# The histogram of the clipped edges, moved from the head of the fourth layer to its closing

## The chip, the cores and the metric

The kernel runs on one core of a Trainium2 chip. The metric is the device time of one execution in microseconds (us); the number compared is the median of several runs. PE is TensorE, DVE is VectorE, ACT is ScalarE, POOL is GpSimd, SP is the engine that issues most transfers.

## The reference, cut to what matters

The network takes four images of 128 channels and 1024 tokens through four layers and a graph step with experts. The fourth layer (`_L3_attn_ref`) is a global attention with 8 heads of 16, a local attention over a window of 5, and two small networks:

```python
x_global = global_mha(x, g_in_w, g_in_b, g_out_w, g_out_b, H_GLOBAL)
x_local = local_mha(x, t_in_w, t_in_b, t_out_w, t_out_b, H_LOCAL)
x_comb = jnp.concatenate([x_global, x_local], axis=-1)
x_fused = jax.nn.silu(x_comb @ fus_w1.T + fus_b1) @ fus_w2.T + fus_b2
x = layer_norm(x + x_fused, gn_g, gn_b)
x_ffn = jax.nn.silu(x @ ffn_w1.T + ffn_b1) @ ffn_w2.T + ffn_b2
x = layer_norm(x + x_ffn, fn_g, fn_b)
```

The graph step behind it softmaxes over the edges that arrive at each of M = 4096 nodes:

```python
e = jax.nn.leaky_relu(a_src[src] + a_dst[dst], negative_slope=0.2)
denom = jax.ops.segment_sum(jnp.exp(e - e_max[dst]), dst, num_segments=M)
```

Edge indices can lie beyond M. A source beyond M is clipped to the last node, so all such edges carry the same message, and the kernel needs of them only how many arrive at each node: a histogram over 4096 nodes, `k.count`.

## The kernel before

**The histogram.** An earlier stage leaves in DRAM (`last_digits`) the target of each clipped edge as two base-64 digits, 1024 slots in each of 128 partitions. For a stretch of slots DVE writes one-hot rows: one `is_equal` for each of the 64 digit values, over both digits at once (`one_hots`, L2510, into `f_hot` or `f_hot_late`). PE multiplies low by high one-hots, two 64x64 products a slot pair, accumulated in PSUM (`multiply`, L2060). A stretch is called a tally. There are nine: five of 128 slots (`EARLY`) ahead of the layer's first image, and four of 96 slots (`LATE`) beside that image. In all 1024 such matmuls and 576 `is_equal`s. A sum over the two halves and a small transposition give `k.count` (L2525, L2086, L2528). It is read only in the graph step.

**The layer** is one stage, `fourth_layer_stream`. Every engine runs its own list in order, and semaphores tie them. The main line is 256 steps, 64 an image. A step makes two score tiles (L2156, PE) into the ring of two PSUM banks, whose row maxima DVE takes (L2492); two transposed score tiles (L2183), of which ACT makes exponentials (L2375); and half a visit of products with the values (L2202, "mix"). The operands of the scores are the stacks, `f_stacks`, loaded by SP from DRAM (L2698, 12 transfers a group of two heads, 48 in the first load).

**Beside it** run smaller programs that yield turn numbers, two turns a step: `pre(b)` (norm, projections and bf16 parts of image b), `local(b)`, and `tail(b)` (output projection, the two networks and three norms of image b). `Beside.turn` lets every program with a due turn issue; programs in the order of their list on ties. `tail(b)` starts at turn 128(b+1), stretched by `TAIL_PACE` 1.1, so `tail(3)` lies behind the last step: the closing. Nothing else but the end of `local(3)` was due there. `tail` uses one PSUM bank, `x0`: PE fills it, ACT or DVE empties it, and only then PE fills it again. The late tallies accumulated in `x0`'s bank, so `tail(0)` waited for `tallied`.

**Ahead of the steps** each engine ends `pre(0)`. Then PE ran the five early tallies into `f_O` (L2071), with one small matmul for `f_o_bias`, and DVE the 320 `is_equal`s for them; then came 32 score tiles with their maxima, then step 0. POOL waited for the early tallies (L2651) before it cleared `f_pads`, which shares their memory. SP loaded the digits (L2717, L2718), then parts and stacks.

## Time and profile before

| | us |
|---|---|
| median of 3 runs | 2576.82 (2575.90 to 2578.19) |
| profiled execution, its own time | 2575.91 |
| its span | 2574.1 |
| PE, DVE, ACT, POOL busy | 1915.4, 1592.9, 1024.6, 723.4 |
| last part of `pre(0)` on PE to first score tile | 1320.8 to 1377.0 |
| first score tile to step 0 | 1377.0 to 1404.4 |
| images 0, 1, 2, 3 (ends of their last group) | 1623.0, 1816.0, 2012.3, 2186.4 |
| the closing (`tail(3)`) | 2186.4 to 2298.4 |
| graph step and experts | to 2574.1 |

The places are in us from the span's start. The own time is 1.8 above the span: what lies around it. Busy shares over the whole span say little here, since each stretch has its own limit; the stretches are read one by one.

### The profile page before, as it was taken

Reading aid. Unit: us, or ns where it says so; the run is one execution under the profiler, and the core shown is the slowest. Engines: PE = TensorE matmul, PEld = TensorE weight load, DVE = VectorE, ACT = ScalarE, POOL = GpSimd, SP = SyncE. Lnnn points to the kernel's source line nnn. Section 1 sums busy time; section 2 is a strip of 40 time slices with the busy share of each in tenths; the row PEclk is TensorE's granted clock in tenths of the full one; section 3 lists DMA queues with packets and bytes.
Section 4 is the critical chain, followed back from the end, with each engine's and each line's share of the span. In section 5 each row is a group of like instructions: output and inputs, shape, how many; then the busy total and the mean of one; then the engine's idle time right before and its main releaser. Section 6 shows DMA issues by size and latency. Waiting matters only on the chain. (4 is left out here: it accounts for less than half of the span.)

```text
span 2574.1 us, 26674 instructions
## 1 busy us (share of the span) xinstructions
PE 1915.4 (74%) x8906; PEld 866.5 (34%) x8906; DVE 1592.9 (62%) x3660; ACT 1024.6 (40%) x1662; POOL 723.4 (28%) x693
## 2 busy tenths in 40 slices
PE   1594786787589566599978889887887887338595
PEld 1121321322233134456654333222322222124355
DVE  3477768768677775547667666566566563115567
ACT  0242142224304116445511544765765665224251
POOL 2300620440171041034450211233233123127730
PEclk7696887789689777789955998998998997659797
DMA  3300300300030000021020010110110100014100
GB/s 97 90 3 25 90 0 19 80 17 19 10 87 1 23 3 0 1 97 20 16 68 15 27 28 15 38 41 15 39 41 15 28 3 4 12 59 52 10 5 34
DMA packets 55807, 80.26 MB, mean 31 GB/s; under 512 B 17217, under 2 KB 28983, under 8 KB 55424
## 3 DMA queue, kind: packets, MB, share of 16 engines
q1 hardware_dynamic: 45158, 69.14, 9.0%
q10 hardware_dynamic: 6426, 7.99, 1.4%
q0 software_dynamic: 4096, 1.58, 1.3%
q8 instruction: 62, 1.02, 0.2%
q14 instruction: 65, 0.53, 0.1%
HBM read 50.13 MB, written 24.68 MB: 29 GB/s over the span
## 5 line engine op out<-in xcount | busy, mean ns | idle before, releaser
L2492 DVE TENSOR_REDUCE f_half_max<-f_ring 128x1 f32<-128x512 f32 x512 | 339.1, 686 | 286.7 <-PE f_ring L2156 284.3
L2375 ACT ACTIVATE f_probs<-f_ST 128x512 f32<-128x512 f32 x512 | 294.6, 597 | 262.6 <-PE f_ST L2183 259.0
L2156 PE MATMUL f_ring<-f_stacks 96*128 96x512 bf16 x512 | 215.3, 422 | 46.1 <-DVE f_half_max L2492 39.9
L772 DVE TENSOR_REDUCE att_half_max<-att_ring 128x1 f32<-128x512 f32 x256 | 161.2, 684 | 101.1 <-PE att_ring L659 92.2
L2183 PE MATMUL f_ST<-f_stacks 99*128 99x512 bf16 x512 | 207.1, 410 | 11.8 <-ACT f_probs L2375 11.8
L755 ACT ACTIVATE att_probs<-att_ST 128x1024 f32<-128x1024 f32 x128 | 129.3, 1023 | 155.9 <-PE att_ST L684 155.7
L2202 PE MATMUL f_O<-f_probs,f_v_ext 128*32 128x512 f32 x1024 | 157.5, 691 | 0.1
L3208 POOL DMA_INDIRECT ti_row<-features,slot_from x128 | 127.0, 992 | 56.4 <-issue 56.4
L659 PE MATMUL att_ring<-stacks 96*128 96x512 bf16 x256 | 104.5, 473 | 47.3 <-DMA stacks<-parts_dram 25.6
L684 PE MATMUL att_ST<-stacks 96*128 96x512 bf16 (+1 forms) x512 | 137.7, 398 | 0.0
L1242 DVE TENSOR_TENSOR loc_weighed<-loc_wide,l_pad 128x512 f32<-128x512 f32 x200 | 124.8, 684 | 19.9 <-PE loc_wide L1196 15.3
L702 PE MATMUL att_O<-att_probs,v_ext 128*64 128x512 f32 x512 | 130.5, 635 | 6.7 <-DVE att_den L791 6.7
L2156 PEld LDWEIGHTS f_ring<-f_stacks 96*128 96x128 bf16 x512 | 50.8, 99 | 249.5 <-DVE f_half_max L2492 168.3
L1739 ACT ACTIVATE bm_h<-bm_ps,bn 128x512 f32<-128x512 f32 x128 | 99.5, 777 | 78.2 <-PE bm_ps L1706 72.9
L1762 POOL TENSOR_TENSOR bm_h<-bm_h,bm_mix 128x512 f32<-128x512 f32 x64 | 82.0, 1303 | 159.6 <-ACT bm_h L1739 88.5
L1224 POOL TENSOR_TENSOR loc_partial<-loc_partial,loc_weighed 128x512 f32<-128x512 f32 x88 | 110.0, 1271 | 15.3 <-DVE loc_weighed L1242 11.8
L1053 POOL MEMSET loc_padded<- 104x1296 f32 x4 | 4.7, 1177 | 387.3 <-POOLq L43 387.3
L1202 PE MATMUL loc_acc<-loc_weighed,turned 128*128 128x512 f32 x208 | 111.2, 619 | 0.0
L2763 PE MATMUL gm_ps<-xn_cm,x 128*128 128x512 f32 x128 | 65.9, 643 | 44.8 <-ACT turned L2811 35.0
L1019 PE MATMUL loc_ps<-loc_prod,place 128*32 128x512 f32 (+1 forms) x208 | 56.8, 713 | 31.2 <-DVE loc_prod L1081 31.2
L2352 ACT CAST f_stacks<-f_ring 3x512 bf16<-3x512 f32 x64 | 36.9, 577 | 97.7 <-PE f_ring L2168 97.2
L684 PEld LDWEIGHTS att_ST<-stacks 96*128 96x128 bf16 (+1 forms) x512 | 49.4, 102 | 75.5 <-issue 17.5
(589 smaller groups left out, 3698.1 us busy)
## 6 DMA issues: line engine op xcount, KB each, us to landing
f_stacks<-f_parts SPq DMA_DIRECT2D x192, 64.0 KB, 2.2
parts_dram<-l_parts SPq DMA_DIRECT2D x8, 768.0 KB, 3.6
stacks<-parts_dram SPq DMA_DIRECT2D x24, 256.0 KB, 9.4
stacks<-parts_dram ACTq DMA_DIRECT2D x24, 256.0 KB, 10.5
f_parts<-f_parts SPq DMA_DIRECT2D x8, 768.0 KB, 3.4
es_raw<-L_ffn_edge_index SPq DMA_DIRECT2D x8, 512.0 KB, 4.1
bm_mix<-mix SPq DMA_DIRECT2D x8, 512.0 KB, 8.7
xn_cm<-x SPq DMA_DIRECT2D x1, 2048.0 KB
```

Of the source, the lines that this page charges most:

```text
L684: last = nc.tensor.matmul(ST[:, s % 2, n * BANK:(n + 1) * BANK], k.stacks[0:rows, 1, per * h + j, m * P:(m + 1) * P], k.stacks[0:rows, 0, ...
L702: last = nc.tensor.matmul(O[at:at + width, :], k.v_ext[:, m, h, :], probs[:, s % probs_ring, n * BANK:(n + 1) * BANK], start=(m == 0), sto ...
L755: nc.scalar.activation(probs[:, s % probs_ring, :], ST[:, s % 2, :], ACT.Exp).then_inc(probs_ready, 1)
L772: nc.vector.tensor_reduce(half_max[:, h % 2, t, n:n + 1], ring[:, i % RING], AX.X, ALU.max, negate=True).then_inc(reduced, 1)
L1202: nc.tensor.matmul(acc[:, n], w_out, weighed[:, (i - LAG) % RING], start=(j == 0), stop=False).then_inc(summed, 1)
L1242: nc.vector.tensor_tensor(o_, a, v, ALU.mult).then_inc(weighed_ready, 1)
L2156: nc.tensor.matmul(ring[:, i % RING], f.stacks[0:STACK, 0, at, t * P:(t + 1) * P], f.stacks[0:STACK, 1, at, n * BANK:(n + 1) * BANK], star ...
L2183: nc.tensor.matmul(ST[:, i % HALVES], f.stacks[0:STACK + 3, 1, h % HEADS, m * P:(m + 1) * P], f.stacks[0:STACK + 3, 0, h % HEADS, n * BANK ...
L2202: last = nc.tensor.matmul(O[at:at + 32, :], f.v_ext[:, h // HEADS % 2, m, h % HEADS, :], f.probs[:, s % PROBS, n * BANK:(n + 1) * BANK], s ...
L2375: nc.scalar.activation(f.probs[:, s % PROBS, n * BANK:(n + 1) * BANK], ST[:, i % HALVES], ACT.Exp).then_inc(probs_ready, 1)
L2492: nc.vector.tensor_reduce(f.half_max[:, h % 2, t, n:n + 1], ring[:, i % RING], AX.X, ALU.max, negate=True).then_inc(reduced, 1)
L3208: self.nc.gpsimd.indirect_dma_start(self.row[:, j, :], None, self.k.features, bass.IndirectOffsetOnAxis(ap=self.k.slot_from[:, j:j + 1], a ...
```

## The change

All nine tallies leave the head of the layer. In their place stand eight tallies of 128 slots in the closing, beside `tail(3)`: 1024 matmuls as before, 512 `is_equal`s. One-hots stand in `f_hot`, two buffers, now laid over `f_stacks` (first buffer) and over `f_v_ext` and `f_probs` (second buffer). So tally 0 waits for the last transposed scores, tally 1 for the last mix, and from tally 2 on DVE waits until PE is done with the buffer. The product stands in the ring's banks, the digits in the second third of `f_xn`, `total` and `place` in `f_qk`. The turns come from a table, `TALLY_TURNS`: DVE makes tally s between entries s and s+1, in pieces of 4 values; PE multiplies it between entries s+1 and s+2, in pieces of 8 matmuls; both are stretched by 1.1 as the tail is. SP's digits transfer is one, at turn 384. `tail(0)`, the first mix, and POOL's clearing of `f_pads` lose their waits.

```diff
-    EARLY, EARLY_TALLIES, LATE, LATE_TALLIES, LATE_TURNS = 128, 5, 96, 4, 28
+    TALLY, TALLIES = 128, 8
+    TALLY_TURNS = (0, 13, 25, 35, 48, 56, 72, 83, 93, 104)
...
+        with ExitStack() as last:
+            self.hot = last.enter_context(sbuf(nc, "f_hot", [P, 2, 2, 2, 64, self.TALLY // 2], BF16))
         self.stacks = sb("f_stacks", [P, 2, self.HEADS, N], BF16)
         self.v_ext = sb("f_v_ext", [P, 2, NT, self.HEADS, 32])
+        self.probs = sb("f_probs", [P, self.PROBS, N])
...
+    def tally_turn(s, share):
+        lo, hi = (f.TALLY_TURNS[min(i, f.TALLIES + 1)] for i in (s, s + 1))
+        return lo + (hi - lo) * share
...
-        if tally is not None:
-            programs.append((0, tally()))
...
+        if tally is not None:
+            programs.append((B * TURNS, paced(tally(), f.TAIL_PACE)))
...
         def first():
-            for s in range(f.EARLY_TALLIES):
-                yield 22 + 2 * s
-                if s == 0:
-                    nc.tensor.matmul(ST[:, 0, 0:1], k.turned[:, k.t_g_out, :], k.cols[:, C_G_IN + 2:C_G_IN + 3],
-                                     start=True, stop=True).then_inc(carried, 1)
-                pe.wait_ge(hot_ready, 64 * (s + 1))
-                multiply(O, f.hot[:, s % 2], range(f.EARLY // 2), s == 0, s == f.EARLY_TALLIES - 1).then_inc(multiplied, 1)
+            yield 22
+            nc.tensor.matmul(ST[:, 0, 0:1], k.turned[:, k.t_g_out, :], k.cols[:, C_G_IN + 2:C_G_IN + 3],
+                             start=True, stop=True).then_inc(carried, 1)
 
         def tally():
-            half, per = f.LATE // 2, 4
-            for s in range(f.LATE_TALLIES):
+            half, per = f.TALLY // 2, 4
+            for s in range(f.TALLIES):
                 for g in range(half // per):
-                    yield f.LATE_TURNS * s + 15 + g
+                    yield tally_turn(s + 1, g * per / half)
                     if g == 0:
-                        pe.wait_ge(hot_ready, 64 * (f.EARLY_TALLIES + s + 1))
+                        pe.wait_ge(hot_ready, 64 * (s + 1))
+                        pe.wait_ge(reduced, count["s"])
+                        pe.wait_ge(rows_off, count["r"])
...
             for n in range(NC2):
                 yield 24 + 2 * n
-                if b == 0 and n == 0:
-                    pe.wait_ge(tallied, 1)
...
-            if v == 0:
-                pe.wait_ge(counted, 2)
...
         before.finish()
-        dve.wait_ge(digits_in, 32)
-        for s in range(f.EARLY_TALLIES):
-            if s >= 2:
-                dve.wait_ge(multiplied, s - 1)
-            one_hots(f.hot[:, s % 2], f.digits[:, :, s * f.EARLY:(s + 1) * f.EARLY], range(64))
-            if s == 2:
-                dve.wait_ge(carried, 1)
...
+        dve.wait_ge(carried, 1)
...
-        pool.wait_ge(multiplied, f.EARLY_TALLIES)
         nc.gpsimd.memset(f.pads[:], 0.0).then_inc(cleared, 1)
...
+        def digits():
+            yield 0
+            normed.wait(sp, 1, 2 * NT)
+            sp.dma_start(f.digits, k.digits_dram).then_inc(digits_in, 16)
```

PE at the head of the layer. Before, with the last matmul of `pre(0)` first (L2005), the early tallies (L2060) and the first score tiles (L2156):

```order
L2005 MATMUL f_side<-turned,xn_cm 128x128 x8
L2068 MATMUL f_ST<-cols,turned 128x1
L2060 MATMUL f_O<-f_hot 64x64 x640
L2156 MATMUL f_ring<-f_stacks 128x512 x32
L2168 MATMUL f_ring<-ident_b,f_shift_parts 3x128 x16
```

Now (the change moves line numbers by a few; L2152 is the score tile):

```order
L2005 MATMUL f_side<-turned,xn_cm 128x128 x8
L2066 MATMUL f_ST<-cols,turned 128x1
L2152 MATMUL f_ring<-f_stacks 128x512 x32
L2164 MATMUL f_ring<-ident_b,f_shift_parts 3x128 x16
```

The 640 matmuls between the two are gone.

PE in the closing, before: output projection (L2117), first network (L2096, L2105), turned tokens (L1985), second network, turned tokens, features (L2142):

```order
L2202 MATMUL f_O<-f_probs,f_v_ext 32x512 x8
L2117 MATMUL f_side<-f_o,turned 128x512 x2
L2096 MATMUL f_side<-f_both,turned 128x512 x8
L2105 MATMUL f_side<-turned,f_hid 128x128 x16
L1985 MATMUL f_side<-ident,f_x_415 128x128 x8
L2096 MATMUL f_side<-xn_cm,turned 128x512 x4
L2105 MATMUL f_side<-turned,f_hid 128x128 x16
L1985 MATMUL f_side<-ident,f_x_415 128x128 x8
L2142 MATMUL f_side<-w_gat,xn_cm 128x24 x8
```

Now the tallies' matmuls (L2060) stand between them. The first part, up to the first turned tokens:

```order
L2060 MATMUL f_ring<-f_hot 64x64 x112
L2113 MATMUL f_side<-f_o,turned 128x512
L2060 MATMUL f_ring<-f_hot 64x64 x32
L2113 MATMUL f_side<-f_o,turned 128x512
L2060 MATMUL f_ring<-f_hot 64x64 x32
L2094 MATMUL f_side<-f_both,turned 128x512 x2
L2060 MATMUL f_ring<-f_hot 64x64 x48
L2094 MATMUL f_side<-f_both,turned 128x512 x2
L2060 MATMUL f_ring<-f_hot 64x64 x56
...
L2103 MATMUL f_side<-turned,f_hid 128x128 x8
L2060 MATMUL f_ring<-f_hot 64x64 x128
```

In the lines left out, the pieces are 32, 56 and 16. The second part, from the second network to the end:

```order
L2060 MATMUL f_ring<-f_hot 64x64 x32
L2094 MATMUL f_side<-xn_cm,turned 128x512
L2060 MATMUL f_ring<-f_hot 64x64 x64
L2103 MATMUL f_side<-turned,f_hid 128x128 x8
L2060 MATMUL f_ring<-f_hot 64x64 x24
L2103 MATMUL f_side<-turned,f_hid 128x128 x8
L2060 MATMUL f_ring<-f_hot 64x64 x280
L1985 MATMUL f_side<-ident,f_x_413 128x128 x8
L2084 MATMUL f_ring<-f_qk 128x32 x2
```

Pieces of 16 and 32 stand ahead of these. No piece stands behind the last 280.

DVE in the closing. Before, from the reciprocal of the softmax sums (L2478) through the first norm:

```order
L2478 RECIPROCAL f_inverse<-f_den 128x64
L2462 SCALAR_TENSOR_TENSOR f_hid<-f_bent,f_straight 128x512 x4
L2472 TENSOR_TENSOR f_xn<-f_side,f_xn 128x512 x2
L2395 BN_STATS f_moments_tail<-f_xn 128x6 x8
L2399 BN_AGGR f_norm_tail<-f_moments_tail 128x2 x8
```

Now, with the one-hots (L2504) between, here from the second residual (L2466) on:

```order
L2466 TENSOR_TENSOR f_xn<-f_side,f_xn 128x512
L2389 BN_STATS f_moments_tail<-f_xn 128x6 x4
L2504 TENSOR_SCALAR f_hot<-f_xn 128x4x64 x8
L2389 BN_STATS f_moments_tail<-f_xn 128x6 x4
L2504 TENSOR_SCALAR f_hot<-f_xn 128x4x64 x4
L2393 BN_AGGR f_norm_tail<-f_moments_tail 128x2 x8
L2504 TENSOR_SCALAR f_hot<-f_xn 128x4x64 x8
```

Twenty one-hots have come between the residual and the end of the first norm's moments; ahead of them, 68 stand before the reciprocal and 104 between it and the first `f_hid`.

## Rows read from the trace of the kernel before

**Rows 1.** Busy time by engine in four stretches, with the granted clock (PEclk).

```profile
core 0: us, PE busy (x) PEld busy (x) DVE busy (x) ACT busy (x) POOL busy (x), PEclk, DMA share, GB/s
1320.00:1377.00 57.00, 54.83 (x646) 54.45 (x646) 30.32 (x193) 2.74 (x3) 23.46 (x5) 0.50 0.27 83
1404.00:1623.00 219.00, 189.50 (x1070) 66.78 (x1069) 147.76 (x492) 106.12 (x186) 35.46 (x31) 0.88 0.07 21
1623.00:1816.00 193.00, 157.40 (x795) 53.69 (x794) 117.42 (x281) 121.97 (x230) 57.15 (x76) 0.96 0.11 32
2186.00:2298.00 112.00, 41.55 (x128) 23.25 (x124) 17.52 (x73) 24.12 (x47) 19.89 (x44) 0.60 0.03 7
```

**Rows 2.** Timeline of PE at the head: start, duration, work, [idle before <- releaser].

```profile
1320.77 21.66 PE L2060 MATMUL f_O<-f_hot 128*64 128x64 bf16 x256
1344.60 32.42 PE L2060 MATMUL f_O<-f_hot 128*64 128x64 bf16 x384 [2.17 <-DVE f_hot L2510]
1376.96 1.03 PE L2156 MATMUL f_ring<-f_stacks 96*128 96x512 bf16 x2
```

**Rows 3.** Timeline of DVE at the head of the layer.

```profile
1295.39 17.62 DVE L2510 TENSOR_SCALAR f_hot<-f_digits 128x256 bf16<-128x256 bf16 x128
1331.81 12.73 DVE L2510 TENSOR_SCALAR f_hot<-f_digits 128x256 bf16<-128x256 bf16 x64 [18.80 <-PE f_O L2060]
1355.67 8.80 DVE L2510 TENSOR_SCALAR f_hot<-f_digits 128x256 bf16<-128x256 bf16 x64 [2.34 <-PE f_O L2060]
1377.60 11.05 DVE L2492 TENSOR_REDUCE f_half_max<-f_ring 128x1 f32<-128x512 f32 x16 [13.13 <-PE f_ring L2156]
```

**Rows 4.** Timeline of SP's queue: the load of the stacks.

```profile
1332.45 24.45 SPq L2698 DMA_DIRECT2D f_stacks<-f_parts  x48
```

**Rows 5.** DMA issues by line at the head: KB each, median us to landing.

```profile
f_stacks<-f_parts SPq DMA_DIRECT2D x48, 64.0 KB, 2.2
```

**Rows 6.** Groups by line and form in image 0: busy, mean ns.

```profile
L2510 DVE TENSOR_SCALAR f_hot_late<-f_xn 128x192 bf16<-128x192 bf16 x256 | 44.1, 239 | 0.0
L2060 PE MATMUL f_side<-f_hot_late 128*64 128x64 bf16 x384 | 42.6, 367 | 0.0
```

**Rows 7.** Timeline of PE in image 0: one piece and what follows it.

```profile
1433.35 0.88 PE L2060 MATMUL f_side<-f_hot_late 128*64 128x64 bf16 x8
1434.16 1.12 PE L1999 MATMUL f_side<-xn_cm,turned 128*128 128x512 f32 x2
```

**Rows 8.** Timeline of ACT: the copies that end image 0 and image 1.

```profile
1623.00 0.58 ACT L2360 COPY f_raw<-f_O 128x512 f32<-128x512 f32 x1 [0.43 <-PE f_O L2202]
1816.00 0.58 ACT L2360 COPY f_raw<-f_O 128x512 f32<-128x512 f32 x1 [0.43 <-PE f_O L2202]
```

**Rows 9.** Timeline of PE in the closing.

```profile
2184.09 2.21 PE L2202 MATMUL f_O<-f_probs,f_v_ext 128*32 128x512 f32 x16
2203.79 2.08 PE L2117 MATMUL f_side<-f_o,turned 128*128 128x512 f32 x2 [17.48 <-POOL f_o L2619]
2209.65 3.54 PE L2096 MATMUL f_side<-f_both,turned 128*128 128x512 f32 x4 [0.87 <-ACT f_both L163]
2214.70 1.96 PE L2096 MATMUL f_side<-f_both,turned 128*128 128x512 f32 x4 [1.51 <-ACT f_straight L163]
2227.98 2.02 PE L2105 MATMUL f_side<-turned,f_hid 128*128 128x128 f32 x16 [0.88 <-DVE f_xn L2472]
2262.48 3.75 PE L2105 MATMUL f_side<-turned,f_hid 128*128 128x128 f32 x16 [0.88 <-DVE f_xn L2472]
2290.42 1.12 PE L1985 MATMUL f_side<-ident,f_x 128*128 128x128 f32 x4 [24.19 <-ACT f_x L2237]
```

**Rows 10.** Timeline of POOL: one subtraction at the head, the softmax scaling in the closing.

```profile
1310.99 4.00 POOL L2587 TENSOR_TENSOR f_qk<-f_qk,f_parts 128x1024 f32<-128x1024 f32 x1 [12.54 <-ACT f_parts L2256]
2201.39 2.34 POOL L2619 TENSOR_TENSOR f_o<-f_o,f_x 128x1024 f32<-128x1024 f32 x1 [27.00 <-DMA f_x<-f_inverses]
```

**Rows 11.** What line L2587 took in all: minimum, median, maximum in ns.

```profile
L2587 POOL TENSOR_TENSOR f_qk<-f_qk,f_parts x8: 2121/2128/4004, 1311.0 to 1860.0; 128x1024 f32<-128x1024 f32 x8
```

More of the change, by code:

```diff
@@ L1829, in __init__ @@
         self.features = sb("f_features", [P, NT, FEAT])
[L1830 to L1838 removed]
+        self.digits = self.xn[:, 1].rearrange("p t n -> p (t n)").bitcast(BF16).rearrange("p (d n) -> p d n", d=2)
+        self.total = self.qk[:, 0, 0:256].rearrange("p (o n q) -> p o n q", o=2, q=2)
+        self.place = self.qk[:, 0, 256:320]
         self.raw = sb("f_raw", [P, 2, BANK])
@@ L1847, in __init__ @@
         self.att_t = sb("f_att_t", [3 * self.ROWS, N], BF16)
-        with ExitStack() as late:
-            self.hot_late = late.enter_context(sbuf(nc, "f_hot_late", [P, 2, 2, 64, self.LATE // 2], BF16))
         self.both = sb("f_both", [P, 2, N])
@@ L2512, in tally @@
         def tally():
-            per = 5
-            for s in range(f.LATE_TALLIES):
+            yield tally_turn(0, 0)
+            split.wait(dve, B - 1)
+            for half in range(2):
+                r = slice(64 * half, 64 * half + 64)
+                nc.vector.tensor_copy(f.place[r, :], k.ident[r, r]).then_inc(tally_made, 1)
+            nc.vector.memset(f.total, 0.0).then_inc(tally_made, 1)
+            dve.wait_ge(digits_in, 16)
+            per = 4
+            for s in range(f.TALLIES):
                 for g in range(0, 64, per):
-                    yield f.LATE_TURNS * s + 1 + g // per
+                    yield tally_turn(s, g / 64)
                     if g == 0:
-                        dve.wait_ge(multiplied, f.EARLY_TALLIES + s)
-                    one_hots(f.hot_late, f.digits_late[:, :, s * f.LATE:(s + 1) * f.LATE], range(g, min(g + per, 64)))
-            yield f.LATE_TURNS * f.LATE_TALLIES + 2
-            dve.wait_ge(multiplied, f.EARLY_TALLIES + f.LATE_TALLIES)
-            dve.wait_ge(counted, 2)
+                        if s == 0:
+                            dve.wait_ge(st_ready, NC2 * len(steps))
+                            dve.wait_ge(reduced, count["s"])
+                        elif s == 1:
+                            dve.wait_ge(mixed_ready, len(steps) // VISIT)
+                        else:
+                            dve.wait_ge(multiplied, s - 1)
+                    one_hots(f.hot[:, s % 2], f.digits[:, :, s * f.TALLY:(s + 1) * f.TALLY], range(g, g + per))
+            yield tally_turn(f.TALLIES + 1, 0) + 2
+            dve.wait_ge(multiplied, f.TALLIES)
+            dve.wait_ge(tally_made, 3)
             for odd in range(2):
-                x = f.total[:, odd, :, odd]
-                nc.vector.tensor_tensor(x, x0.psum[:, 0:64], x, ALU.add).then_inc(counted, 1)
-            yield f.LATE_TURNS * f.LATE_TALLIES + 6
+                nc.vector.tensor_copy(f.total[:, odd, :, odd], ring[:, 0, 0:64]).then_inc(counted, 1)
+            yield tally_turn(f.TALLIES + 1, 0) + 6
             dve.wait_ge(spread_out, 1)
-            nc.vector.tensor_copy(k.count[:], x0.psum[:, 64:64 + MT]).then_inc(tallied, 1)
+            nc.vector.tensor_copy(k.count[:], ring[:, 1, 0:MT]).then_inc(tallied, 1)
         def laps():
```

32 lines of the change are left out of this document (7 added, 25 removed).

## Prediction, made before the changed kernel was run

> **What bounds the kernel now.** No engine is busy over the whole span, so the reader goes stage by stage: busy times by stretch, then the timelines of the engines that wait there. Three stretches carry the histogram or will.
>
> At the head of the layer PE and DVE hand tallies to each other, and PE is the slower. It runs 256 matmuls in 21.66 us and 384 in 32.42 [rows 2]: 0.0845 us each, 10.8 for a tally of 128. DVE makes 64 one-hots in 8.8 us, 0.1375 each, and otherwise waits for PE, 18.80 us once [rows 3]. The first score tile starts at 1376.96, on the heels of the last tally matmul [rows 2]. The stacks that it reads were loaded long before: SP issued 48 transfers in 24.45 us from 1332.45 [rows 4], each landing 2.2 us after its issue [rows 5]. So this stretch is paced by the histogram alone.
>
> In image 0 both PE (189.5 of 219 us) and DVE (147.8) are fuller than in image 1 (157.4 and 117.4 of 193), though image 1 has a tail beside it and image 0 has none [rows 1]. The surplus is the late tallies.
>
> In the closing all engines are nearly empty: PE 41.6 of 112 us, DVE 17.5 [rows 1]. It is one chain, PE, ACT, DVE, POOL in turn, with gaps on PE from 0.88 us inside the networks to 17.48 and 24.19 ahead of the output projection and the last turned tokens [rows 9].
>
> **Part 1, the head: -36.3 us.** Gone from PE are 640 matmuls, from DVE 320 one-hots. What is late next is the load of the first group's 12 transfers. SP issues one each 24.45/48 = 0.51 us, the twelfth at 1332.45 + 11 x 0.51 = 1338.1; issued by 1338.5 and landed 2.2 later, at 1340.7 [rows 4, 5]. The first score tile starts there and not at 1376.96 [rows 2]: 36.3 saved. The 32 tiles and their maxima keep their pace, 11.05 us for 16 on DVE [rows 3]. The remaining 36 transfers end near 1359, and step 0, at 1404.4 - 36.3 = 1368, is the first to want the second group. SP's own queue loses two digit transfers ahead of `pre(0)`; the parts' transfers wait for POOL, so nothing moves. POOL clears `f_pads` earlier, and nobody waits for it. Bounds: 34 if the transfers land as late as 1343; 37 if the load is a little faster.
>
> **Part 2, image 0: -44 us.** Gone are 48 pieces of 8 matmuls. A piece takes 0.81 us to the next start [rows 7]: 48 x 0.81 = 38.9 on PE. DVE loses 256 one-hots, 44.1 us busy [rows 6]. They lie side by side, so at most the larger counts in full. Image 0's steps take 1623.0 - 1404.4 = 218.6 us [rows 8]. From PE's side: 218.6 - 38.9 = 180 if its 30 us of waiting stay, and some of that waiting is for maxima that stood behind one-hots. From DVE's side 218.6 - 44.1 = 174.5. From a like image: image 1 took 193.0 [rows 8] with `pre`, `local` and a tail; the tail's PE work in the closing is 41.6 us, mostly at half clock [rows 1], so 20 to 25 at full clock; that leaves 168 to 173. I take 174.5: 44 saved. Bounds: 26, if image 0 only falls to image 1's 193, and 52, if it reaches 167.
>
> **Part 3, the closing: +41 us.** This is the sum with the most in it, and I walk through PE's list as it is built. PE has 1024 x 0.0845 = 86.5 us of tallies to place beside 41.6 of tail [rows 1, 2]. Idle there are 70 us, but they must be idle at the right places, since PE runs in order: a projection whose input is ready waits for the piece in front of it.
> - Tally 0: DVE may start at the last transposed scores, 2184.2 [rows 9], and needs 8.8; PE starts it at 2193.0 and has run 112 matmuls (9.5 us) by 2202.5, ahead of the projection at 2203.79 [rows 9]. It costs nothing: it fills the 17.48.
> - POOL's scaling at 2201.39 [rows 10] now meets DVE's one-hots of tally 1, which run to 2202.6. In the head the same meeting cost POOL: 4.00 us for an instruction with a median of 2.13 [rows 10, 11], ending 2 us after DVE's burst of 17.62 us from 1295.39 [rows 3]. So it starts at 2202.6: +1.2.
> - Output projection and first network: between these eight operations stand 32, 32, 48, 56, 32, 56 and 16 tally matmuls, 272 x 0.0845 = 23.0 us. The operations are two projections of 2.08, four of 3.54 and two of 3.75 at half clock [rows 9]: 25.8. PE never waits in here, so the stretch lasts 48.8. Before it lasted 2230.00 - 2203.79 = 26.2 [rows 9]: +22.6.
> - First norm on DVE: 8, 4 and 8 one-hots between its instructions, 20 x 0.1375: +2.8. Beside the norm PE runs tally 3 (10.8) in a gap of at least 12: nothing.
> - Second network: here gaps of 1.51 (0.88 ahead of the last) face pieces of 16 and 32 at the turned tokens (+1.7), three of 32, each 2.7 against 1.51 plus 0.35 of overlap with the end of the operation before (+0.9 each, +2.7), 64 (+4) and 24 (+1.3): +9.7.
> - Second norm: 28 one-hots (3.9) and a wait until PE is done with tally 5 (1.3): +5.1.
> - Tallies 6 and 7, 256 matmuls or 21.6 us on PE, fall into the 24.19 ahead of the last turned tokens [rows 9]: nothing. They end some 5 us before the tokens are there. If that cover were gone, each us over it would count in full.
>
> 1.2 + 22.6 + 2.8 + 9.7 + 5.1 = 41.4. Bounds: 23, with the clock as in the first rival, and 50, if each of some 17 re-entries costs the 0.81 - 8 x 0.0845 = 0.13 us that a piece in image 0 costs over the steady rate [rows 2, 7] and POOL loses a burst of 0.1375 x 36 = 5 to DVE once more.
>
> The new digits transfer on SP at turn 384 lands during image 3, 100 us and more before it is read; queued behind it are the moves of one group, which wait for PE anyway. Nothing.
>
> **Sum.** Own time 2575.9 - 36.3 - 44 + 41.4 = 2537.0; the median of the runs is 0.9 above that execution. **Forecast 2538 us.**
>
> **The clock, and a page that speaks for more.** The tally matmuls did not raise PE's clock: from 1320 to 1377 it was busy for 54.8 of 57 us with them and the granted clock was 0.50 throughout, the level of 1.2 GHz [rows 1]. In the closing it rose once, after the four-matmul projection at 2209.65: 3.54 us before it and 1.96 after for the same form [rows 9]. I therefore price the tail's operations at half clock throughout. The Trainium skill, "TensorE: Matmul & The Clock Gate", section "Why this matters for your kernels", says that an engine kept continuously busy gets and keeps the full clock. By it the closing, where PE now hardly idles, would run at 2.4 GHz. The trace does not agree for these narrow matmuls; whether mixed with wide ones they let it rise, no row of the closing shows.
>
> **The port, and a page.** In the head, a POOL instruction was held until DVE's one-hots ended (above), which is where my 1.2 us come from. The Trainium skill, "SBUF — State Buffer", section "Who interferes with whom", says that the second to issue is blocked until the first instruction finishes, a single instruction. By it POOL would wait for one one-hot, 0.1 us, and the sum would be 1.1 lower. The row has 1.9 us, and I follow it.
>
> **Rivals.**
> - *The clock comes back in the closing.* Mixed with wide projections the pieces may let it rise; in image 0 pieces ran at full clock, 1.12 us for a projection right behind one [rows 7]. Then the first stretch loses four times 3.54 - 1.96 and twice 3.75 - 2.02 and half of the two projections, 11.6 us, and the second network about 7: closing +23. 2519 us. Against it stands the head's 0.50. 17%.
> - *Image 0 is held by its other chain.* `pre(1)` and `local(0)` pass one bank between PE, ACT, DVE and POOL, at a speed that tallies do not set. Then it falls only to image 1's 193.0: 26 instead of 44. 2556 us. Against it: image 1 has a tail as well. 13%.
> - *The load is late.* If the first tiles in fact waited for all 48 transfers, to 1359, the head gives 18: 2556 us. The change would not do what it says there. PE's wait names 12 only. 5%.
> - *Slower: nothing hides.* PE runs strictly in order. If each tally delays the chain by its full length, because one-hots and matmuls are each ready only when the next operation of the tail is too, then the closing costs 86.5 + 8.8 = 95, 15 more than the 80 that parts 1 and 2 give: 2592 us. It decides from the point where less than 15 us of tally work fall into idle time. The 17.48 and 24.19 [rows 9] alone hold 31. 4%.
>
> **How the numbers follow.** Forecast 61%, its own range 2524 to 2550 (image 0 by 8 either way, the closing by 9). The range that should hold 8 in 10 reaches to the clock's 2519 and to the 2556 of the two middle rivals, with a little for the tails: 2514 to 2558. A measurement of this kernel can tell about 0.2%, 5 us. All cases but the last and a small middle lie far below: faster 0.95, same 0.01, slower 0.04.
>
> **What would show it.** First score tile near 1341; step 0 near 1368; image 0 ending near 1543, the closing starting near 2106 and lasting 153 instead of 112; PE without idle time between the output projection and the second projection of the network, at a granted clock near 0.50; tally 7 over some 5 us before the last turned tokens. I am wrong if image 0 lasts 190 or more, if PE waits for one-hots inside the networks, if the last tally runs into the last turned tokens, or if the clock is at 1.00 in there.

## Result and the profile after

The changed kernel takes 2506.8 us (median of 4 runs, 2505.3 to 2514.1) against 2577.5 (median of 4, 2575.9 to 2581.1): a ratio of 0.9729, interval 0.9707 to 0.9751, or 70.7 us less. The forecast was 2538, its range 2514 to 2558. The sign was right, and the gain was 31 us larger than foretold.

The profiled execution takes 2505.7 us, its span is 2503.9. The two spans, cut at the same events (first norm of the layer on DVE, first ACT exponential of the attention, the last copy of O of each image, the last copy of features):

| stretch | before, us | after, us | difference | forecast |
|---|---|---|---|---|
| ahead of the layer | 1290.4 | 1285.1 | -5.3 | 0 |
| head | 114.7 | 77.3 | -37.4 | -36.3 |
| image 0 | 217.9 | 159.5 | -58.4 | -44 |
| image 1 | 193.0 | 193.1 | +0.1 | 0 |
| image 2 | 196.3 | 196.2 | -0.1 | 0 |
| image 3 | 174.0 | 167.7 | -6.3 | 0 |
| closing | 111.7 | 148.1 | +36.4 | +41.4 |
| behind the layer | 276.1 | 276.8 | +0.7 | 0 |
| span | 2574.1 | 2503.9 | -70.2 | -38.9 |

Busy time by engine in the head up to the first score tile, in image 0, image 1, image 3 and the closing of the changed kernel (compare [rows 1]):

```profile
core 0: us, PE busy (x) PEld busy (x) DVE busy (x) ACT busy (x) POOL busy (x), PEclk, DMA share, GB/s
1285.10:1334.20 49.10, 14.75 (x34) 7.42 (x34) 4.22 (x21) 12.24 (x20) 21.64 (x19) 0.54 0.15 50
1361.70:1521.90 160.20, 136.76 (x681) 36.87 (x680) 105.93 (x232) 103.11 (x186) 34.62 (x31) 0.95 0.09 28
1521.90:1715.10 193.20, 158.36 (x795) 53.99 (x795) 117.45 (x282) 122.01 (x231) 57.16 (x76) 0.95 0.11 32
1911.30:2078.90 167.60, 142.87 (x702) 45.96 (x700) 89.68 (x228) 106.24 (x202) 46.02 (x59) 0.92 0.05 13
2078.90:2227.40 148.50, 131.54 (x1152) 111.64 (x1152) 86.00 (x574) 24.70 (x48) 24.25 (x44) 0.65 0.02 6
```

The timeline of PE at the head, after (compare [rows 2]): the wait is now for the stacks' load, as foretold.

```profile
1315.06 0.43 PE L2066 MATMUL f_ST<-cols,turned 128*128 128x1 f32 x2
1334.24 1.03 PE L2152 MATMUL f_ring<-f_stacks 96*128 96x512 bf16 x2 [18.76 <-DMA f_stacks<-f_parts]
```

The timeline of SP's queue there, after, up to 1337 us (compare [rows 4]):

```profile
1326.89 10.43 SPq L2689 DMA_DIRECT2D f_stacks<-f_parts  x22
```

The timeline of POOL there, after: the subtraction that took 4.00 us [rows 10] is back at the line's median [rows 11], since no one-hots run beside it.

```profile
1305.64 2.12 POOL L2579 TENSOR_TENSOR f_qk<-f_qk,f_parts 128x1024 f32<-128x1024 f32 x1 [12.52 <-ACT f_parts L2250]
```

The timeline of PE in the closing, after (compare [rows 9]):

```profile
2085.64 9.64 PE L2060 MATMUL f_ring<-f_hot 128*64 128x64 bf16 x112 [6.76 <-DVE f_hot L2504]
2097.28 2.08 PE L2113 MATMUL f_side<-f_o,turned 128*128 128x512 f32 x2 [2.00 <-POOL f_o L2611]
...
2107.05 3.78 PE L2094 MATMUL f_side<-f_both,turned 128*128 128x512 f32 x4
2110.76 4.29 PE L2060 MATMUL f_ring<-f_hot 128*64 128x64 bf16 x48
2114.98 3.44 PE L2094 MATMUL f_side<-f_both,turned 128*128 128x512 f32 x4
2118.35 4.94 PE L2060 MATMUL f_ring<-f_hot 128*64 128x64 bf16 x56
2123.22 3.15 PE L2094 MATMUL f_side<-f_both,turned 128*128 128x512 f32 x4
2126.30 2.89 PE L2060 MATMUL f_ring<-f_hot 128*64 128x64 bf16 x32
2129.12 1.98 PE L2094 MATMUL f_side<-f_both,turned 128*128 128x512 f32 x4
...
2143.00 10.92 PE L2060 MATMUL f_ring<-f_hot 128*64 128x64 bf16 x128
2154.97 1.12 PE L1985 MATMUL f_side<-ident,f_x 128*128 128x128 f32 x4 [1.05 <-ACT f_x L2231]
...
2203.89 10.97 PE L2060 MATMUL f_ring<-f_hot 128*64 128x64 bf16 x128 [1.10 <-DVE f_hot L2504]
2219.44 1.11 PE L1985 MATMUL f_side<-ident,f_x 128*128 128x128 f32 x4 [4.59 <-ACT f_x L2231]
```

From the output projection at 2097.28 no row carries a wait until 2154.97: every operation of the network now stands behind a piece of tallies, and the last tally ends 4.6 us ahead of the last turned tokens. Both were foretold. What was not is the same form, four wide matmuls, in 3.78, 3.44, 3.15 and 1.98 us. The granted clock says why: it changes between its two levels, 0.50 (1.2 GHz) and 1.00 (2.4 GHz), while PE never pauses; a figure between them is the mean of both. Over the first and second of the four, and over a piece and the fourth:

```profile
2107.05:2110.83 3.78, 3.78 (x8) 1.24 (x6) 0.00 (x0) 0.00 (x0) 0.00 (x0) 0.50 0.00 0
2114.98:2118.35 3.37, 3.37 (x7) 0.96 (x5) 0.66 (x5) 0.00 (x0) 0.00 (x0) 0.56 0.03 5
2126.30:2129.12 2.82, 2.82 (x34) 2.72 (x33) 1.33 (x7) 1.29 (x2) 0.00 (x0) 1.00 0.01 3
2129.12:2131.03 1.91, 1.91 (x6) 0.67 (x5) 1.91 (x16) 0.00 (x0) 0.00 (x0) 1.00 0.00 0
```

Over the third it was 0.61, over the pieces between the first three 0.86 and 0.85.

Three entries of the table were to be explained: image 0 (14 us more than forecast), the closing (5 us less added than forecast) and two stretches that the change does not touch, ahead of the layer and image 3, 11.6 us together.

### The profile page after: what moved, and what is told of

The parts are those of the page before. It is cut to its first block and busy times, and to the rows that moved or that the text cites. A ratio compares the mean times of both kernels' runs of the same rounds, so it can differ in the third digit from the quotient of the medians.

```text
span 2503.9 us, 26613 instructions
## 1 busy us (share of the span) xinstructions
PE 1892.9 (76%) x8906; PEld 869.7 (35%) x8906; DVE 1573.4 (63%) x3594; ACT 1021.7 (41%) x1662; POOL 714.1 (29%) x693
## 5 line engine op out<-in xcount | busy, mean ns | idle before, releaser
L2152 PE MATMUL f_ring<-f_stacks 96*128 96x512 bf16 x512 | 212.1, 415 | 54.5 <-DVE f_half_max L2486 28.1
L2152 PEld LDWEIGHTS f_ring<-f_stacks 96*128 96x128 bf16 x512 | 50.4, 99 | 258.8 <-DVE f_half_max L2486 162.6
L659 PE MATMUL att_ring<-stacks 96*128 96x512 bf16 x256 | 103.7, 471 | 46.5 <-DMA stacks<-parts_dram 25.9
L2060 PE MATMUL f_ring<-f_hot 128*64 128x64 bf16 x1024 | 90.5, 366 | 7.9 <-DVE f_hot L2504 7.9
L2060 PEld LDWEIGHTS f_ring<-f_hot 128*64 128x64 bf16 x1024 | 87.1, 272 | 22.4 <-issue 12.7
L2504 DVE TENSOR_SCALAR f_hot<-f_xn 128x256 bf16<-128x256 bf16 x512 | 72.3, 220 | 28.7 <-issue 14.7
```

The lines of the kernel that those rows point to most:

```text
L2060: last = nc.tensor.matmul(bank[64 * a:64 * a + 64, 0:64], low, high, start=(start and m == ms[0]), stop=(stop and m == ms[-1]), tile_posit ...
L2152: nc.tensor.matmul(ring[:, i % RING], f.stacks[0:STACK, 0, at, t * P:(t + 1) * P], f.stacks[0:STACK, 1, at, n * BANK:(n + 1) * BANK], star ...
```

## Experiments on image 0: do the two engines' tallies lie side by side, or add?

The forecast rested on the sentence that PE's matmuls and DVE's one-hots lie side by side, "so at most the larger counts in full". Three kernels made from the one before take the late tallies apart. In `late_none` both edits are made, in each of the others one. PE's edit leaves one pair of matmuls of each tally, on the identity:

```diff
                 for g in range(half // per):
                     yield f.LATE_TURNS * s + 15 + g
...
-                    last = multiply(x0.psum, f.hot_late, range(per * g, per * (g + 1)), s == 0 and g == 0,
-                                    s == f.LATE_TALLIES - 1 and g == half // per - 1)
+                    if g < half // per - 1:
+                        continue
+                    for a in range(2):
+                        last = nc.tensor.matmul(x0.psum[64 * a:64 * a + 64, 0:64], k.ident_b[:, 0:64], k.ident_b[:, 0:64],
+                                                start=(s == 0), stop=(s == f.LATE_TALLIES - 1), tile_position=(0, 64 * a))
```

DVE's edit leaves one instruction of the 64 (in `late_matmuls_only` the first tally stays whole):

```diff
-                    one_hots(f.hot_late, f.digits_late[:, :, s * f.LATE:(s + 1) * f.LATE], range(g, min(g + per, 64)))
+                    if g == 0:
+                        nc.vector.tensor_scalar(f.hot_late[:, :, :, 0, :], ..., 0.0, None,
+                                                ALU.is_equal).then_inc(hot_ready, 64)
```

**late_none.**

> The kernel before, with the four late tallies of image 0 left out but for one pair of matmuls and one one-hot instruction of each; the five early tallies at the head stay, and the count is wrong for it. Image 0 (from the first to the last carry-off of O, with the head of its step 0) lasted 218.6 us before and 160.2 in the changed kernel. If the 58.4 us are the late tallies' own price, it lasts 160 here too, and the time is 2576 - 58 = 2518 us. If part of them came from elsewhere (other addresses of the tiles, the bank that the tail shared, waits that went), it lasts 170 to 180 and the time is 2528 to 2538.

**late_hots_only.**

> The kernel before, with the late tallies' matmuls left out but for one pair of each; their 256 one-hots stay. Theory: score tile and maximum hand two banks to each other, so a piece on PE and a piece on DVE delay the same loop in turn and their prices add; without the matmuls image 0 falls by about 33, to 185, and the time to 2543 us. Rival 1, as forecast: they lie side by side and the larger one counts, PE's; then nearly all of it goes, image 0 is near 165 and the time 2522. Rival 2: it is the one-hots, which hold POOL and are held by it; then little goes, image 0 stays above 205 and the time above 2562.

**late_matmuls_only.**

> The kernel before, with all 384 late matmuls, but the one-hots of the second to the fourth late tally left out (one instruction of 64 stays), three quarters of DVE's work; those of the first stay. Theory that the prices add: with 25 us of one-hots for the whole and three quarters gone, image 0 falls by 19, to 200, the time to 2557 us. Rival 1 (side by side, PE the larger): nothing falls, 215 to 219, 2573 us or more. Rival 2 (the one-hots cost most): it falls by 35 or more, to 183, 2541 us or less.

Measured were 2523.2, 2546.3 and 2559.5 us, one execution each; the kernel before took 2573.4 beside them. Image 0 lasted 162.1, 186.3 and 204.4 us.

Busy time by engine over image 0, first the kernel before:

```profile
1405.10:1623.00 217.90, 188.40 (x1067) 66.54 (x1068) 146.93 (x491) 106.12 (x186) 35.46 (x31) 0.88 0.07 21
```

without the late tallies (`late_none`):

```profile
1404.20:1566.30 162.10, 139.80 (x691) 38.72 (x691) 107.07 (x239) 103.24 (x186) 34.65 (x31) 0.93 0.09 28
```

with one-hots alone (`late_hots_only`):

```profile
1400.10:1586.40 186.30, 150.82 (x691) 39.50 (x692) 144.51 (x490) 104.04 (x186) 35.28 (x31) 0.86 0.08 24
```

and with matmuls and one tally's one-hots (`late_matmuls_only`):

```profile
1399.60:1604.10 204.50, 185.79 (x1067) 66.27 (x1068) 116.95 (x302) 105.79 (x187) 34.99 (x31) 0.89 0.07 22
```

Against 162.1 the one-hots alone cost 24.2 us, the matmuls with a quarter of the one-hots 42.3, and both together 55.8. The larger alone is not the whole: most of the smaller price comes on top. The theory that the prices add said 185 and 200, measured were 186.3 and 204.4; the forecast's rule wanted 165 and 215 or more. The sum isn't exact: three quarters of the one-hots were worth 13.5 us beside the matmuls, where three quarters of 24.2 are 18.

The rows above say what each price consists of. If every PE instruction is counted from its start to the next one's, the 384 late matmuls fill 39.2 us, in the kernel before and in `late_matmuls_only` alike. Against `late_none`, in us:

| | one-hots | matmuls | both |
|---|---|---|---|
| late matmuls on PE | 0 | 39.2 | 39.2 |
| all other work of PE | +11.0 | +6.8 | +9.4 |
| idle time of PE | +13.2 | -3.7 | +7.2 |
| image 0 | +24.2 | +42.3 | +55.8 |

So the matmuls hardly use the 22.3 us in which PE is idle without them, and the one-hots add idle time.

How a one-hot on DVE costs time on a stage that PE bounds is in PE's groups over image 0 (busy, mean ns of one, idle ahead of it and its cause). The score tiles in `late_hots_only`:

```profile
L2159 PE MATMUL f_ring<-f_stacks 96*128 96x512 bf16 x134 | 58.0, 433 | 20.4 <-DVE f_half_max L2495 18.3
```

and in `late_none`:

```profile
L2159 PE MATMUL f_ring<-f_stacks 96*128 96x512 bf16 x134 | 55.3, 413 | 8.4 <-DVE f_half_max L2495 5.9
```

PE waits 18.3 us for maxima that stand behind one-hots, instead of 5.9. And it works more slowly: the same 691 matmuls take 150.82 us at a granted clock of 0.86 and 139.80 at 0.93. So of the 24.2 us 13.2 are idle time, nearly all of it these waits, and 11.0 are longer matmuls. Which of the two draws the other, whether the waits pull the clock down, was not tried apart; the rows show them together in every kernel here.

The same split for the change itself: PE was busy for 188.40 of 217.9 us before, and the late matmuls took 39.2 of it. (The 42.6 of [rows 6] count the end of each piece too, which overlaps with the start of what follows, as in [rows 7].) Afterwards it is busy for 136.06 of 159.5, as the row of the changed kernel cut at these events says:

```profile
1362.40:1521.90 159.50, 136.06 (x679) 36.77 (x679) 105.23 (x231) 103.09 (x186) 34.62 (x31) 0.95 0.09 28
```

39.2 are the matmuls; 188.40 - 39.17 - 136.06 = 13.2 come from nearly the same work, at a clock of 0.95 instead of 0.88; and idle time fell by 29.5 - 23.4 = 6.1. The sum is the 58.4 of the table. `late_none` shows that 55.8 of them are the late tallies' own; the other 2.6 go with what else the change took out of image 0 (that kernel still has the stand-in pieces and the waits of the shared bank), not told apart further.

## Experiments on the closing: whose price is it, and what is the clock's part?

Three kernels made from the changed one do the same to the closing's eight tallies, with the same two edits (in `closing_matmuls_only` the first two tallies keep their one-hots).

**closing_none.**

> The changed kernel, with the tallies of the closing left out but for one pair of matmuls and one one-hot instruction of each. The closing lasted 112.0 us before and 148.1 in the changed kernel. If the tallies cost their 36 there, it lasts 112 and the time is 2506 - 36 = 2470 us. If the changed kernel's closing is quicker or slower by itself (other banks, no shared bank), it shows as a length other than 112. Images 1 to 3 and what lies ahead of the layer are the same code as in the changed kernel: if image 3's 167.7 us (174.0 before) and the 5.3 us ahead of the layer are properties of the code, they come again; if they differ from run to run, this shows by how much.

**closing_hots_only.**

> The changed kernel, with the closing's tally matmuls left out but for one pair of each tally; its 512 one-hots stay. Without any tallies the closing lasts 112.1 us, with all 148.1. Theory: the one-hots cost there only what stands in the two norms and the meeting with POOL, 2.6 + 3.9 + 0.9 us, so it lasts 120 us and the time is 2479. Rival: prices add as in image 0 and a good part of the 36 is DVE's; then it lasts 128 or more, 2487 us or more. The POOL scaling before the output projection, 2.34 us alone and 3.33 in the changed kernel, should be 3.3 here if DVE's one-hots hold it, and 2.34 if it is PE's or a transfer's doing.

**closing_matmuls_only.**

> The changed kernel, with all 1024 tally matmuls in the closing, but the one-hots of the third to the eighth tally left out (one instruction of 64 stays). Theory: PE's order makes the price, 19.6 us in the first network, 7.9 in the second; norms and POOL lose nothing, so the closing lasts 112 + 28 = 140 us, 2498 us. Rival: without the one-hots the closing falls by the whole of what a 120 us closing with one-hots alone leaves, to 140 as well, but with PE idle inside the networks; then the two engines' prices are not additive there. Tallies 6 and 7 end with the chain's own gap ahead of the last turned tokens unfilled by 7 to 9 us instead of 4.6.

Measured were 2471.8, 2478.1 and 2503.7 us. The closing by stretches, each from the start of one PE operation to the next, in us:

| stretch | none | one-hots | matmuls | both (changed kernel) | split_2_6, below |
|---|---|---|---|---|---|
| to the output projection | 17.8 | 18.5 | 18.4 | 18.3 | 18.2 |
| projection and first network | 25.9 | 27.0 | 46.7 | 45.7 | 30.9 |
| first norm | 9.4 | 11.9 | 10.9 | 12.0 | 12.0 |
| second network | 26.9 | 25.1 | 36.2 | 34.8 | 26.7 |
| second norm to the last turned tokens | 24.5 | 28.9 | 26.4 | 29.7 | 28.4 |
| to the features | 7.6 | 7.6 | 7.6 | 7.6 | 7.6 |
| closing | 112.1 | 119.0 | 146.2 | 148.1 | 123.8 |

Without tallies the closing is what it was before, 112.1 against 111.7, so the 36 us are the tallies'. One-hots alone cost 7 us, where 8 were expected. Matmuls alone cost 34.1, where 28 were expected: I had left out that they lengthen the norms too (1.5 and 1.9 us), and each network was over 1 us dearer than in the changed kernel (20.8 against 19.8 and 9.3 against 7.9), since its operations took that much longer. PE was not idle inside the networks, and it waited 2.85 us ahead of the last turned tokens, where 7 to 9 were expected. Both together cost 36.0, not 41: three quarters of the one-hots are worth 1.9 us beside the matmuls. So here, far more than in image 0, the two do lie side by side. That DVE prepares one tally ahead, so that mostly the order on PE counts, is the likely reason; it was not tried apart.

The timeline of PE in `closing_none`, two operations with the stand-in piece between them:

```profile
2111.49 1.96 PE L2097 MATMUL f_side<-f_both,turned 128*128 128x512 f32 x4 [1.51 <-ACT f_straight L163]
2113.37 0.22 PE L2081 MATMUL f_ring<-ident_b 128*64 128x64 bf16 x2
2114.95 1.95 PE L2097 MATMUL f_side<-f_both,turned 128*128 128x512 f32 x4 [1.36 <-ACT f_straight L163]
```

The gap is 1.5 us, and the pieces of the changed kernel are 2.9 to 5.0 us long in the first network, all but the last (1.6). Counted from start to start, its seven pieces fill 24.1 us, where the gaps of `closing_none` (with the stand-in pieces) are 8.9; and its operations take 21.6 instead of 17.1 us, at the lower clock. So the 19.8 us of the first network are 15.3 of pieces longer than their gaps and 4.5 of slower operations. In the second network the pieces are 11.8 longer than the gaps, and the operations take 3.8 less than in `closing_none` (13.9 instead of 17.7): 7.9.

Two more rows settle a smaller matter, who holds whom on POOL and DVE. The multiplication of the first norm takes 2.38 us in `closing_none`, and in the changed kernel

```profile
2156.54 5.22 POOL L2617 TENSOR_TENSOR f_xn<-f_x,wide 128x1024 f32<-128x1024 f32 x1 [3.31 <-ACT f_x L2231]
```

beside DVE's

```profile
2149.22 10.17 DVE L2504 TENSOR_SCALAR f_hot<-f_xn 128x256 bf16<-128x256 bf16 x72
```

DVE's burst ends at 2159.39, and POOL ends 2.37 us behind it, at 2161.76. With one-hots alone it takes 5.09, with hardly any (`closing_matmuls_only`) 2.48. POOL's scaling ahead of the output projection, 2.34 in `closing_none`, takes 3.17 with one-hots alone, so they hold it and not the matmuls. In `closing_matmuls_only` the other case shows: the single one-hot instruction that DVE starts 0.05 us after POOL's takes 2.52 us instead of 0.14, the length of POOL's.

```profile
2157.00 2.48 POOL L2622 TENSOR_TENSOR f_xn<-f_x,wide 128x1024 f32<-128x1024 f32 x1 [3.32 <-ACT f_x L2231]
...
2157.05 2.52 DVE L2529 TENSOR_SCALAR f_hot<-f_xn 128x256 bf16<-128x256 bf16 x1 [7.25 <-PE f_ring L2060]
```

## What the untouched stretches do by themselves

With the experiments and the versions below there are twelve profiles, all with the same code ahead of the layer. The first norm of the layer starts on DVE at 1290.40 before and 1285.07 after, and in the kernel without late tallies and the one with one-hots alone in the closing at:

```profile
1289.68 1.65 DVE L2398 BATCH_NORM_STATS2 f_moments_pre<-t_tm 128x6 f32<-128x128 f32 x8 [0.32 <-PEq L43]
```

```profile
1281.63 1.64 DVE L2392 BATCH_NORM_STATS2 f_moments_pre<-t_tm 128x6 f32<-128x128 f32 x8 [0.32 <-PEq L43]
```

The twelve reach from 1281.6 to 1290.4, and two of the kernel before's three variants lie at 1285. Between the traces of before and after the largest single step, 2.6 us, lies near 497 us, in the local attention of an earlier layer; what sets it off was not found. The changed kernel was profiled once more:

**after_again.**

> The changed kernel once more. If the 5.3 us that it was ahead at the start of the layer and its short image 3 (167.7 us against 174.0) are chance of an execution, this profile shows other values, between 1281 and 1291 us for the first norm's start and 167 to 176 us for image 3, and the time is 2505 to 2515 us. If they are its own, they come again to 0.3 us. Head, image 0 and closing should come again in either case: 49.2 us from the first norm to the first score tile, 159.5 and 148.1.

It took 2507.4 us (2501.9 to 2511.2), 0.9733 of the kernel before, interval 0.9717 to 0.9749. The layer started at 1285.25, image 3 lasted 170.0, image 0 159.5 and the closing 147.4. Image 3 was 167.6 to 175.5 us long over the twelve, and 171.4 to 175.5 in the three variants of the kernel before. The three kernels of the closing, whose image 3 is the changed kernel's, had 173.3 to 174.8. So image 3's 6.3 us are largely the execution's. They go with the clock: the same 702 matmuls keep PE busy for 142.87 us at 0.92 in the changed kernel (its row for image 3 stands above), and before for 146.74 at 0.89.

```profile
2012.34:2186.37 174.03, 146.74 (x702) 47.31 (x700) 87.23 (x209) 106.34 (x202) 45.97 (x59) 0.89 0.05 12
```

Ahead of the layer variants of both kernels share the range as well; that the changed kernel came to 1285.1 and 1285.25 leaves open whether a part of the 5.3 is its own. Image 0, by contrast, was 159.5 to 159.8 in every kernel that has no late tallies at all.

## A version that beats both

The tables say where a tally is free: where PE is idle for long and DVE's one-hots are ready. The head after the change has PE idle for 18.76 us and DVE for longer. `split_2_6` keeps the first two tallies there and six in the closing. The one-hots of the head lie over the ring of probabilities and what follows it, as before; `f_parts`, `f_qk` and `f_lq` go under the closing's one-hots:

```diff
-    TALLY, TALLIES = 128, 8
-    TALLY_TURNS = (0, 13, 25, 35, 48, 56, 72, 83, 93, 104)
+    TALLY, TALLIES, EARLY = 128, 6, 2
+    TALLY_TURNS = (0, 13, 25, 48, 56, 83, 93, 104)
...
+            for s in range(f.EARLY):
+                yield 22 + 2 * s
+                pe.wait_ge(hot_ready, 64 * (s + 1))
+                multiply(O, f.hot_early[:, s % 2], range(f.TALLY // 2), s == 0, s == f.EARLY - 1).then_inc(multiplied, 1)
...
+        dve.wait_ge(multiplied, f.EARLY)
+        nc.vector.tensor_copy(f.part[:], O[:, 0:64]).then_inc(counted, 1)
```

**split_2_6.**

> The whole histogram, in two parts: two tallies of 128 at the head of the layer, in buffers that lie over the ring of probabilities and what follows it, and six in the closing. DVE makes the two head tallies' one-hots while pre(0) still runs, PE multiplies them from about 1315 us on for 21.6 us and ends at 1337, where it would otherwise wait for the stacks' load until 1334. Cost at the head 3 us, and up to 2 more because the one-hots hold POOL in front of the parts' transfer. The closing loses two tallies that stood inside the networks: first network 12 us shorter, second 5 to 6. Sum: 2507 - 18 + 4 = 2493 us. Rival: the head costs what it gives (POOL held for 2 us or more, transfers late, then the maxima), 2505 or more. Rival: the remaining pieces leave the clock low in the networks and the gain is halved, 2500.

**split_3_5.**

> As split_2_6, with three tallies at the head and five in the closing. The third at the head is bare: 10.8 us on PE with nothing to hide it. In the closing it takes one more out, the one that stood in the gap ahead of the last turned tokens, where it cost nothing. By the theory that only the tallies without an idle stretch of PE cost, it is 10 us slower than split_2_6, 2503. If the price of a tally in the closing were even, 36/8 = 4.5 us each, it would be 6 us slower, 2499.

`split_2_6` took 2484.3 us (2482.3 to 2493.0), 0.9640 of the kernel before, interval 0.9605 to 0.9676: 93 us less than before and some 23 less than the change (the intervals of the two ratios do not meet). The timeline of PE at its head:

```profile
1316.11 21.44 PE L2065 MATMUL f_O<-f_hot_early 128*64 128x64 bf16 x256
1337.48 1.03 PE L2161 MATMUL f_ring<-f_stacks 96*128 96x512 bf16 x2
```

The first score tile comes 51.8 us after the first norm instead of 49.2: two tallies cost 2.6 us there. In the closing they were worth 24.3, where I expected 18. Its timeline of PE in the first network:

```profile
2112.35 3.78 PE L2103 MATMUL f_side<-f_both,turned 128*128 128x512 f32 x4
2116.07 2.25 PE L2065 MATMUL f_ring<-f_hot 128*64 128x64 bf16 x24
2118.25 1.99 PE L2103 MATMUL f_side<-f_both,turned 128*128 128x512 f32 x4
2120.16 2.30 PE L2065 MATMUL f_ring<-f_hot 128*64 128x64 bf16 x24
2122.39 1.98 PE L2103 MATMUL f_side<-f_both,turned 128*128 128x512 f32 x4
```

Pieces of 16 to 24 matmuls nearly fit the gaps of 1.5 us, and the wide operations take 1.99 and 1.98 us from the second on. 144 matmuls in the first network cost 5.0 us, where 272 cost 19.8: the pieces are 4.6 longer than the gaps, and the operations only 0.3 slower. 120 in the second network seem to cost nothing (26.7 against 26.9), but that is two things at once: the pieces are 2.4 longer than the gaps, and the operations take 2.6 less than in `closing_none` (15.1 instead of 17.7), because the clock stood higher for some of them. Of the 6 us by which the closing beat the expectation, the first network has nearly 3 (14.8 for 12), the second 2 to 3 (8.1 for 5 to 6), and the second norm 1.3.

`split_3_5` took 2501.0 us (2493.5 to 2504.6), 0.9697, interval 0.9661 to 0.9733. In its profile the head is 13.4 us longer than `split_2_6`'s (93.3 against 79.9) and the closing 3.8 shorter (120.0): 9.6 us, near the 10 expected, but made up otherwise. At the head the third tally costs its 11.0 us on PE and 2.37 of waiting for its one-hots. In the closing the tally taken out was not free: the second norm is 4.0 us shorter (24.4, what it lasts with no tallies), close to the even price of 4.5 that was the other expectation. The rest of the 17 us between the medians isn't accounted for; in the two profiles, 12.6 us apart, it is 3 us, and image 3 alone differs by 5.8 there (173.4 against 167.6), within the range that it has by itself.

**split_fit.**

> split_2_6 with the turn table of the closing shifted a little: tally 0 runs 120 instead of 112 matmuls ahead of the output projection, and the first norm's gap takes 112 instead of 128, the second network 16 more. If a piece costs only what it is longer than the gap between two operations, this saves 0.7 us ahead of the projection and 1.3 in the norm and loses 0.6 in the second network: 1.4 us less than split_2_6, 2483, not to be told apart by the time, but by the stretches of the trace. If the price went by the number of pieces or by the clock alone, the stretches stay or the second network loses 2 us or more.

It took 2493.8 us (2483.9 to 2497.1), 0.9662, interval 0.9639 to 0.9686: not better, and by the time not to be told from `split_2_6`. Its closing lasted 125.4 us. The first network was 1.1 us shorter than `split_2_6`'s, for 0.7 meant. The norm stayed at 12.0, though PE now waited 2.33 us in it: there DVE's one-hots set the length, not PE's tally, which the expectation had wrong. The second network lost 2.0 us with 16 more matmuls, where the surplus of a piece was put at 0.6: 1.4 are the pieces, with no gap left for them, and 0.6 is one operation that took 3.78 us instead of 3.20. The 2.0 was named as the sign that the clock has a part in the price, and it has.

## Why the prediction was wrong, point by point

- **The head, -36.3.** Right. The load of the first group became the last event, and the first score tile came 37.4 us sooner after the first norm, a little past the bounds of 34 to 37. Of the 1.1 us more, about 0.6 is the pace, 5.0 us from the first issue to the twelfth instead of 5.6; 0.2 is an earlier start of the load after the norm, and the rest is that the twelfth transfer landed 2.3 us after its issue, where the sum had 2.6.
- **Image 0, -44.** This is the step that failed: "They lie side by side, so at most the larger counts in full." It was 58.4, outside its bounds of 26 to 52. The 44 taken was DVE's busy time; read from PE's side it is the 38.9 of matmuls and 5.1 of waits. The matmuls filled 39.2 and the waits gave 6.1. But the longer duration of all other matmuls of image 0 while the late tallies lay beside them, at the lower clock, 13.2 us, was in no term, though [rows 1] has 0.88 for image 0 beside 0.96 for image 1. 0.3, 1.0 and 13.2 are, but for rounding, the 14.4 that were missing. What the experiments show in place of the step: 24.2 us for the one-hots alone, 42.3 for the matmuls with a quarter of them, 55.8 for both, so the larger was no ceiling; each engine's tallies lengthened PE's other work (by 11.0 and 6.8), and the one-hots added 13.2 of waits. The likeness with image 1 was no safe bound either: image 0 without tallies takes 159.5, and 193 less a tail was put at 168 to 173.
- **The closing, +41.4.** Right in its mechanism, 36.4 measured. By its own terms: start 1.2 (0.5 by the stretches), first network 22.6 (19.8), first norm 2.8 (2.6), second network 9.7 (7.9), second norm 5.1 (5.2). The two networks are short by 4.6, and that hides two misses of opposite sign. The operations took about 4 us less in each network than priced, which is the clock: the four wide ones of the first were priced at 3.54 throughout and took 3.78, 3.44, 3.15 and 1.98. The pieces cost 1.1 and 2.1 us more than priced; those of the first network fill 24.1 us instead of 23.0.
- **The clock.** "Half clock throughout" was too low and the rival's "comes back" too high: 0.73 from the output projection to the end of the first network, where 0.50 was the sign named, and 0.65 over the closing. The Trainium skill, "TensorE: Matmul & The Clock Gate", section "Why this matters for your kernels", says that continuous work gets and keeps the full clock. The trace does not agree: over the 57.7 us from 2097.28 to 2154.97, in which PE paused once, for 1.05, stretches of 10 us were granted 0.50, 0.68, 0.83, twice 0.84 and, at the end of a run of 128 narrow matmuls, 0.50 again:

```profile
2099.00:2109.00 10.00, 10.00 (x70) 6.92 (x70) 6.08 (x44) 1.41 (x2) 0.00 (x0) 0.50 0.01 2
2109.00:2119.00 10.00, 10.00 (x63) 5.95 (x63) 3.41 (x21) 1.75 (x3) 0.00 (x0) 0.68 0.01 2
2119.00:2129.00 10.00, 10.00 (x88) 7.95 (x86) 5.15 (x31) 2.09 (x4) 0.00 (x0) 0.83 0.00 1
2149.00:2159.00 10.00, 8.95 (x88) 7.98 (x88) 9.97 (x72) 4.16 (x10) 5.32 (x14) 0.50 0.01 2
```

- **The port.** POOL's scaling in the closing lost 1.0 us (3.33 against 2.34), 1.2 were foretold from the row at the head. The Trainium skill, "SBUF — State Buffer", section "Who interferes with whom", has the second to issue blocked for the whole of the first instruction. The trace shows a whole burst of them: POOL's 5.22 us ended its own 2.37 behind the last of 72 one-hots.
- **What no step could hold.** 11.6 us of the 31 lie ahead of the layer and in image 3, where the executions of the same code differ by 9 and 8 us. Taken off, the change is worth some 59 us between the two profiles, while the medians differ by 70.7; how much of the 11.6 the medians hold can't be said. Without them the forecast would have been 20 us off, 14.4 of it from image 0, 5.0 from the closing and 1.1 from the head.
- **The range.** Image 0's and the closing's misses went the same way, and the low end was set by the clock rival alone, with image 0 at its forecast.

## What to carry to other kernels

Where two engines hand a ring of two banks to each other, work added to either can delay the loop, and the larger price is no ceiling: here 24.2 and 42.3 us apart made 55.8 together. In the closing, where one engine runs a chain and the other mostly prepares ahead, the price was nearly the one engine's (34.1 of 36.0, with a quarter of the one-hots in it). Price filler by its pieces: each costs what it is longer than the gap that it stands in, and beside that ask what it does to the speed of the operations around it; in the first network these were 15.3 and 4.5 us. And before work is moved off one place entirely, ask how much of it that place hides once it is gone: the head had room for two tallies at 2.6 us, which cost 24 in the closing.

## What was not expected of the hardware

- A narrow tally matmul takes 0.086 us where 0.50 was granted (9.64 us for 112 at 2085.64) and 0.090 where 1.00 was (2.89 us for 32 at 2126.30), while a wide network operation takes 3.78 or 1.98. Filler of this form costs the same at either level.
- The clock in image 0 differs with the tallies beside it: 0.93 without them (`late_none`), 0.88 with both, 0.86 with one-hots alone, which put no work on PE; the same 691 matmuls take 11.0 us longer at 0.86 than at 0.93.
- In the closing the granted clock changed level several times while PE ran without a pause from 2097.28 to 2153.92: 0.50, 0.56, 0.61 and 1.00 over the four wide operations, 0.53 from 2135.90 to 2139.50, 1.00 from there to 2146.00 and 0.51 in the next 3 us.
- Here an instruction of POOL that started inside a burst of DVE's one-hots ended its own length after the burst (5.22 us for 2.37), and one of DVE that started just behind POOL's lasted as long as it (2.52 us for 0.14).
